# Second attention layer: relative rows and score pieces of at most 256 columns put between the transposes of the current tile

## The chip, the cores and the metric

The kernel runs on one core of one Trainium2 chip. The metric is the device time of one execution in microseconds (us). Times in the profile are microseconds from the start of the profiled execution, unless marked ns. Engines: PE is TensorE's matmul side, PEld its weight loads, DVE VectorE, ACT ScalarE, POOL GpSimd, SP SyncE, which issues the DMAs.

## The reference, cut to what matters

Four layers run one after the other on x of shape (2, 1024, 128), each with a layer norm before and after and a residual: attention with 16 heads and shared logits, a mixture of 8 experts, attention with relative positions, and a feed-forward of composed weights. The change is in the third, called the second attention layer here:

```
q = (x @ Wq.T) as (B, 16 heads, T, 8);  k, v with 4 groups, each repeated for 4 heads
scores = (q / sqrt(8)) @ k
dist = clip(pos_k - pos_q, -127, 127) + 127
bias[b,h,q,k] = (q / sqrt(8))[b,h,q] . E[dist[q,k]]
attn = softmax(scores + bias);  out = (attn @ v) @ Wo.T
```

T is 1024, so the bias depends on the position only in a band of 255 distances around the diagonal; outside of it, it is one of two constants per query.

## The kernel before, in words

Function `attend` computes one batch element of this layer, and is called twice. It goes over 16 heads, and in each over 8 tiles of 128 queries: 128 tiles a call, 256 in all. `u = 8h + qt` numbers them. What happens to a tile:

1. `scores` (L331): TensorE multiplies the tile's queries (each number split into three bf16 parts, so the contraction is 72 rows) with all 1024 keys into psS. psS is 128 x 1024 f32 and there is one copy. Three variants of the keys lie in KT: the plain ones for the band, and two with the far constants folded in, for the columns left and right of it. `segments(qt)` says which columns use which variant, cut at 512 as well: 3 or 4 matmuls a tile, 26 a head. Before the first it waits for `s_z >= u`, that is, for VectorE to have read the scores of the tile before. The last one raises `s_s`.
2. VectorE (L439) adds the bias A to psS, writes Z (two copies) and takes the row minimum m (queries are negated), and raises `s_z`.
3. GpSimd (L467, L468) computes m - Z in place, and raises `s_sub`.
4. TensorE (L385) transposes Z in eight blocks of 128 columns with the f32 identity, four into each half of psT. Each half waits for ScalarE to have read it for the tile before, and raises `s_t` when done.
5. ScalarE (L496) takes the exp of each half into Pt (two copies), and raises `s_exp`.
6. `values` (L360) multiplies with the values on TensorE, 32 columns of weights at a time, one tile later.
7. In tiles 3 and 7 of a head, `to_rows` (L371) also folds four tiles' outputs; this document calls them fold tiles.

The bias band is made one head ahead. `relative(h + 1, qt, u + 8)` (L346) multiplies the next head's queries with the 512 rows of the band into psE, one copy of 128 x 512 f32. It waits for `s_rows >= u + 8`: ScalarE must have copied the previous psE. ScalarE's `gather` (L488) copies psE to `rows`, after both exps of the tile, and raises `s_rows`; SyncE stores it to DRAM and fetches it skewed into A, for use one head later. The last head of a batch has no relative matmul.

Each engine goes through its own instructions in the order written. TensorE's order in the loop over tiles (`head`) is: wait for `s_sub`; transposes of half 0, then of half 1; `scores` of tile u + 2; `relative` of tile u + 8; `values` of tile u - 1; the fold where there is one. ScalarE's is: exp of half 0, exp of half 1, copy of psE.

Of the kernel before, what the change touches and what calls it, by code (L numbers as in the profile page):

```python
# [6 lines left out]
P = 128  # L7
# [3 lines left out]
QT_N = N // P  # L11
H, DH = 16, 8
SPLIT = 3
KR = SPLIT * SPLIT * DH
# [278 lines left out]
def attend(nc, tag, b, QT, KT, gkv, V, A, attn, con, segments, rel=None):  # L293
# [8 lines left out]
    RPT = H // gkv  # L302
    idf, fold = con["idf"], con["fold"]
    with phase(nc, tag) as ph:
# [8 lines left out]
        psS = ph.pb("psS", [P, N])  # L313
# [13 lines left out]
        with nc.Block() as block:  # L327

            @block.tensor
            def _(pe):  # L330
                def scores(h, qt, u):  # L331
                    if not (type(u) is int and u == 0):

                        pe.wait_ge(s_z, u)
                    for var, k0, k1 in segments(qt):
                        kh = h if gkv == H else var * gkv + h // RPT
                        last = nc.tensor.matmul(psS[:, k0:k1], QT[0:KR, h, qt * P:(qt + 1) * P], KT[0:KR, kh, k0:k1],  # L337
                                                start=True, stop=True)
                    last.then_inc(s_s, 1)

                def relative(h, qt, v):

                    if not (type(v) is int and v == 0):

                        pe.wait_ge(s_rows, v)
                    nc.tensor.matmul(psE[:], QT[0:KR, h, qt * P:(qt + 1) * P], EBT[0:KR, :], start=True, stop=True).then_inc(s_e, 1)  # L346

                def values(h, qt, u, first):
                    g, t = qt // GS, qt % GS
                    if qt == 0:  # L350

                        pe.wait_ge(s_vh, h + 1)
                    if t == 0 and not first:

                        pe.wait_ge(s_os, h * 2 + (g - 1))

                    pe.wait_ge(s_exp, u * 2 + 2)
                    for kt in range(QT_N):
                        j = kt % 4
                        last = nc.tensor.matmul(psO[32 * j:32 * j + 32, g, t * P:(t + 1) * P], Vh[:, kt, :],  # L360
                                                Pt[:, qt % 2, kt * P:(kt + 1) * P], start=kt < 4, stop=kt >= 4)
                    last.then_inc(s_pv, 1)

                def to_rows(h, g, first=False):


                    pe.wait_ge(s_os, h * 2 + (g + 1))
                    if not first:
                        pe.wait_ge(s_div, h * 2 + g)
                    for t in range(GS):  # L370
                        last = nc.tensor.matmul(psF[:, t, 0:DH + 1], Os[:, g, t * P:(t + 1) * P], fold[:], start=True, stop=True)  # L371
                    last.then_inc(s_f, 1)

                def head(h, first=False, final=False):
                    for qt in range(QT_N):
                        u = h * QT_N + qt

                        pe.wait_ge(s_sub, u + 1)
                        for half in range(2):
                            if not (first and qt == 0):  # L380

                                pe.wait_ge(s_exp, u * 2 + (half - 1))
                            for k in range(4):
                                kt = half * 4 + k
                                last = nc.tensor.transpose(psT[:, half, k * P:(k + 1) * P], Z[:, qt % 2, kt * P:(kt + 1) * P], idf[:])  # L385
                            last.then_inc(s_t, 1)
                        if qt + 2 < QT_N:
                            scores(h, qt + 2, u + 2)
                        elif not final:
                            scores(h + 1, qt + 2 - QT_N, u + 2)  # L390
                        if rel and not final:
                            relative(h + 1, qt, u + QT_N)
                        if qt:
                            values(h, qt - 1, u - 1, first)
                        elif not first:
                            values(h - 1, QT_N - 1, u - 1, first)
                        if qt == 3 and not first:
                            to_rows(h - 1, 1)
                        if qt == 7:
                            to_rows(h, 0, first)  # L400

                if rel:
                    for qt in range(QT_N):
                        relative(0, qt, qt)
                scores(0, 0, 0)
                scores(0, 1, 1)
                head(0, first=True)
                with pe.Fori(1, H - 1) as h:
                    head(h)
                head(H - 1, final=True)  # L410
                values(H - 1, QT_N - 1, H * QT_N - 1, False)
                to_rows(H - 1, 1)
# [1089 lines left out]
```

## Time and profile before

| | |
|---|---|
| median of three runs | 1898.95 us (1897.33 to 1901.57) |
| the profiled execution | 1901.43 us |
| its span, first to last instruction | 1899.7 us |
| mean granted TensorE clock | 0.907 of full |
| busy: PE, PEld | 1552.7 us (82%), 1119.6 us (59%) |
| busy: DVE, ACT, POOL | 1053.9 (55%), 892.1 (47%), 821.5 (43%) |
| relative matmuls, L346 | 256, 101.2 us |
| score matmuls, L337 | 832, 157.5 us |

The attention of the second layer runs from about 1092 to 1424 and from about 1478 to 1810. "Busy" of PE adds the time in which at least one matmul is recorded, from its start to its modelled end; since one starts while another ends, a PE that is always busy may still have gaps in its stream. The groups of the profile name what ended an engine's idle time; "issue" means nothing that the profile shows. A weight load is a row of its own (PEld), started ahead of its matmul where it can be.

### The profile page before, as it was taken

What the parts mean: (1) busy time and instruction counts of PE and PEld (TensorE: products, weight loads), DVE (VectorE), ACT (ScalarE), POOL (GpSimd) and SP (SyncE); (2) the same over time, 40 slices, a digit from 0 to 9 for tenths busy, and PEclk for the clock granted to TensorE, in tenths of its full rate; (3) what the DMA queues carried; (4) which work ended last, traced back from release to release, by engine and by line L of the source; (5) the groups of instructions that cost most, each with busy time, mean ns of one, the idle gap of its engine ahead of it and who ended that gap; (6) DMA issues with size and microseconds to landing.
All of it is one profiled execution on the core that took longest, in us unless ns stands there. A gap on an engine that the chain in (4) does not pass through costs nothing. (4 is left out here: it accounts for less than half of the span.)

```text
span 1899.7 us, 46841 instructions
## 1 busy us (share of the span) xinstructions
PE 1552.7 (82%) x16823; PEld 1119.6 (59%) x16823; DVE 1053.9 (55%) x3049; ACT 892.1 (47%) x1558; POOL 821.5 (43%) x1298
## 2 busy tenths in 40 slices
PE   3799999879999993267970589999995899999935
PEld 2476666646766763145650457777774577777734
DVE  5666556476655655732324845666558455566552
ACT  2355455445555551002220367777753566666612
POOL 2266566426665640062450245555541355555500
PEclk9899999999999995588995789999996799999968
DMA  4000000000000000712531056555530555555400
GB/s 120 1 1 2 2 2 2 2 1 1 2 2 2 2 2 5 251 40 54 104 60 32 1 179 185 178 178 178 175 121 1 161 177 179 182 180 177 138 1 22
DMA packets 102762, 147.48 MB, mean 78 GB/s; under 512 B 11632, under 2 KB 59120, under 8 KB 102640
## 3 DMA queue, kind: packets, MB, share of 16 engines
q1 hardware_dynamic: 95856, 140.87, 23.8%
q0 software_dynamic: 6784, 4.87, 1.9%
q8 instruction: 90, 1.47, 0.3%
q14 instruction: 32, 0.26, 0.0%
HBM read 68.49 MB, written 77.21 MB: 77 GB/s over the span
## 5 line engine op out<-in xcount | busy, mean ns | idle before, releaser
L439 DVE CUSTOM_DVE_ANT_0 t_Z<-t_psS,a1b_A 128x1024 f32<-128x1024 f32 x256 | 312.4, 1220 | 202.3 <-issue 202.3
L657 DVE CUSTOM_DVE_ANT_0 t_Z<-t_psS,a0b_L 128x1024 f32<-128x1024 f32 x256 | 311.1, 1220 | 186.3 <-issue 183.0
L715 ACT ACTIVATE t_Pt<-t_psT 128x512 f32<-128x512 f32 x512 | 278.7, 595 | 253.8 <-PE t_psT L613 253.6
L496 ACT ACTIVATE t_Pt<-t_psT 128x512 f32<-128x512 f32 x512 | 278.3, 595 | 191.9 <-PE t_psT L385 191.9
L613 PE MATMUL t_psT<-idf,t_Z 128*128 128x128 f32 x2048 | 285.8, 284 | 8.1 <-issue 6.6
L680 POOL TENSOR_SCALAR t_Z<-t_Z,t_m 128x1024 f32<-128x1024 f32 x256 | 287.3, 1122 | 0.0
L468 POOL TENSOR_SCALAR t_Z<-t_Z,t_m 128x1024 f32<-128x1024 f32 x256 | 286.8, 1120 | 0.0
L385 PE MATMUL t_psT<-idf,t_Z 128*128 128x128 f32 x2048 | 282.0, 281 | 2.0 <-POOL t_Z L468 1.6
L613 PEld LDWEIGHTS t_psT<-idf,t_Z 128*128 128x128 f32 x2048 | 226.6, 144 | 59.4 <-issue 32.1
L385 PEld LDWEIGHTS t_psT<-idf,t_Z 128*128 128x128 f32 x2048 | 227.7, 144 | 42.5 <-issue 37.4
L467 POOL TENSOR_TENSOR t_touch<-t_m 128x1 f32<-128x1 f32 x256 | 49.4, 193 | 270.1 <-DVE t_m L439 268.2
L360 PE MATMUL t_psO<-t_Pt,t_Vh 128*32 128x128 f32 x4096 | 164.9, 279 | 0.0
L587 PE MATMUL t_psO<-t_Pt,t_Vh 128*32 128x128 f32 x4096 | 164.5, 280 | 0.3 <-ACT t_Pt L715 0.3
L488 ACT ACTIVATE t_rows<-t_psE 128x512 f32<-128x512 f32 x256 | 152.9, 597 | 16.7 <-PE t_psE L346 15.7
L570 PE MATMUL t_psS<-a0b_KT,a0b_QT 72*128 72x512 bf16 (+1 forms) x512 | 155.9, 387 | 5.7 <-PEq L74 4.1
L337 PE MATMUL t_psS<-a1b_KT,a1b_QT 72*128 (+4 forms) x832 | 157.5, 303 | 2.7 <-DVE t_m L439 2.7
L587 PEld LDWEIGHTS t_psO<-t_Pt,t_Vh 128*32 128x32 f32 x4096 | 97.0, 109 | 105.8 <-issue 81.6
L360 PEld LDWEIGHTS t_psO<-t_Pt,t_Vh 128*32 128x32 f32 x4096 | 96.3, 109 | 84.7 <-ACT t_Pt L496 56.7
L679 POOL TENSOR_TENSOR t_touch<-t_m 128x1 f32<-128x1 f32 x256 | 49.4, 193 | 195.3 <-DVE t_m L657 195.0
L346 PE MATMUL t_psE<-a_EBT,a1b_QT 72*128 72x512 bf16 x256 | 101.2, 395 | 13.8 <-ACT t_rows L488 10.0
L256 POOL COPY p_Kx<-p_parts 128x384 bf16<-128x384 bf16 (+1 forms) x96 | 43.9, 493 | 130.8 <-DVEq L231 130.8
L1161 POOL DMA_INDIRECT token_sums<-x_oe,x_xe x40 | 62.3, 1559 | 79.9 <-DVE x_oe L1026 67.7
(252 smaller groups left out, 1766.9 us busy)
## 6 DMA issues: line engine op xcount, KB each, us to landing
relative_rows<-t_rows SPq DMA_DIRECT2D x256, 256.0 KB, 2.0
a1b_A<-relative_rows SPq DMA_DIRECT2D x192, 192.0 KB, 2.5
a1b_A<-relative_rows SPq DMA_DIRECT2D x64, 128.0 KB, 2.3
x_B<-in_b SPq DMA_DIRECT2D x1, 4096.0 KB, 19.3
x_A<-in_a SPq DMA_DIRECT2D x1, 4096.0 KB, 26.7
expert_rows<-zp SPq DMA_DIRECT2D x1, 2740.0 KB, 12.7
x_xe<-expert_rows SPq DMA_DIRECT2D x8, 342.5 KB, 2.9
x_WP<-in_moe_pre SPq DMA_DIRECT2D x8, 256.0 KB, 3.4
```

Of the source, the lines that this page charges most:

```text
L337: last = nc.tensor.matmul(psS[:, k0:k1], QT[0:KR, h, qt * P:(qt + 1) * P], KT[0:KR, kh, k0:k1], start=True, stop=True)
L360: last = nc.tensor.matmul(psO[32 * j:32 * j + 32, g, t * P:(t + 1) * P], Vh[:, kt, :], Pt[:, qt % 2, kt * P:(kt + 1) * P], start=kt < 4, s ...
L385: last = nc.tensor.transpose(psT[:, half, k * P:(k + 1) * P], Z[:, qt % 2, kt * P:(kt + 1) * P], idf[:])
L439: nc.vector.tensor_tensor_reduce(out=Z[:, qt % 2, :], in0=psS[:], in1=A[:, qt, :], scale=1.0, scalar=3e38, op0=ALU.add, op1=ALU.min, accum ...
L468: nc.gpsimd.tensor_scalar(Z[:, qt % 2, :], Z[:, qt % 2, :], -1.0, m[:, qt % 2:qt % 2 + 1], ALU.mult, ALU.add).then_inc(s_sub, 1)
L496: nc.scalar.activation(Pt[:, qt % 2, half * (N // 2):(half + 1) * (N // 2)], psT[:, half, :], ACT.Exp).then_inc(s_exp, 1)
L570: last = nc.tensor.matmul(psS[:, j % 2, k0:k0 + 512], QT[0:KR, hq * J + j, qt * P:(qt + 1) * P], KT[0:KR, hq * J + j, k0:k0 + 512], start= ...
L587: last = nc.tensor.matmul(psO[32 * j:32 * j + 32, (qt % GRP) * P:(qt % GRP + 1) * P], Vh[:, kt, j, :], Pt[:, qt % 2, j, kt * P:(kt + 1) * ...
L613: last = nc.tensor.transpose(psT[:, half, k * P:(k + 1) * P], Z[:, j, kt * P:(kt + 1) * P], idf[:])
L657: nc.vector.tensor_tensor_reduce(out=Z[:, j, :], in0=psS[:, j % 2, :], in1=L[:, qt, :], scale=1.0, scalar=3e38, op0=ALU.add, op1=ALU.min, ...
L680: nc.gpsimd.tensor_scalar(Z[:, j, :], Z[:, j, :], -1.0, m[:, j:j + 1], ALU.mult, ALU.add).then_inc(s_sub, 1)
L715: nc.scalar.activation(Pt[:, qt % 2, j, half * (N // 2):(half + 1) * (N // 2)], psT[:, half, :], ACT.Exp).then_inc(s_exp, 1)
```

## The change: what it does

In `head`, the score matmuls of tile u + 2 and the relative matmul of tile u + 8 are no longer behind the eight transposes of tile u but between them. The segments are cut into pieces of at most 256 columns: 4 pieces in tiles 0 and 7 of a head, 5 in the others, 38 a head. The relative matmul goes behind the first transpose. The pieces go behind the last four or five transposes, one behind each, the last piece behind the eighth. The wait for `s_z` is at the first piece, `s_s` is raised by the last, `s_t` still by the fourth transpose of each half. What is computed is the same.

```diff
+                def pieces(qt):
+                    return [(var, k, min(k + 256, k1)) for var, k0, k1 in segments(qt) for k in range(k0, k1, 256)]
+
+                def scores(h, qt, u, part):
+                    if part == 0 and not (type(u) is int and u == 0):
                         pe.wait_ge(s_z, u)
-                    for var, k0, k1 in segments(qt):
-                        kh = h if gkv == H else var * gkv + h // RPT
-                        last = nc.tensor.matmul(psS[:, k0:k1], QT[0:KR, h, qt * P:(qt + 1) * P], KT[0:KR, kh, k0:k1],
-                                                start=True, stop=True)
-                    last.then_inc(s_s, 1)
+                    var, k0, k1 = pieces(qt)[part]
+                    kh = h if gkv == H else var * gkv + h // RPT
+                    ins = nc.tensor.matmul(psS[:, k0:k1], QT[0:KR, h, qt * P:(qt + 1) * P], KT[0:KR, kh, k0:k1], start=True, stop=True)
+                    if part == len(pieces(qt)) - 1:
+                        ins.then_inc(s_s, 1)
...
                             for k in range(4):
                                 kt = half * 4 + k
                                 last = nc.tensor.transpose(psT[:, half, k * P:(k + 1) * P], Z[:, qt % 2, kt * P:(kt + 1) * P], idf[:])
-                            last.then_inc(s_t, 1)
-                        if qt + 2 < QT_N:
-                            scores(h, qt + 2, u + 2)
-                        elif not final:
-                            scores(h + 1, qt + 2 - QT_N, u + 2)
-                        if rel and not final:
-                            relative(h + 1, qt, u + QT_N)
+                                if k == 3:
+                                    last.then_inc(s_t, 1)
+                                if kt == 0 and rel and not final:
+                                    relative(h + 1, qt, u + QT_N)
+                                part = kt - QT_N + len(pieces((qt + 2) % QT_N))
+                                if part >= 0 and qt + 2 < QT_N:
+                                    scores(h, qt + 2, u + 2, part)
+                                elif part >= 0 and not final:
+                                    scores(h + 1, qt + 2 - QT_N, u + 2, part)
```

Before the first head, the scores of tiles 0 and 1 are now issued in pieces too.

## Rows read from the trace of the kernel before

**Rows 1.** Busy time by stage: span, PE, PEld, DVE, ACT, POOL, clock, DMA.
```profile
1200.00:1220.00 20.00, 20.00 (x254) 14.75 (x256) 12.09 (x39) 14.95 (x27) 10.89 (x19) 1.00 0.58 178
```

**Rows 2.** Order of time, one tile: start, us, engine, line, operation, xcount, idle before.
```profile
1210.42 1.09 PE L385 MATMUL t_psT<-idf,t_Z 128*128 128x128 f32 x8
...
1211.11 1.09 ACT L496 ACTIVATE t_Pt<-t_psT 128x512 f32<-128x512 f32 x2 [0.56 <-PE t_psT L385]
...
1211.35 0.60 PE L337 MATMUL t_psS<-a1b_KT,a1b_QT 72*128 x4
...
1211.79 0.38 PE L346 MATMUL t_psE<-a_EBT,a1b_QT 72*128 72x512 bf16 x1
1212.01 1.22 DVE L439 CUSTOM_DVE_ANT_0 t_Z<-t_psS,a1b_A 128x1024 f32<-128x1024 f32 x1 [1.02 <-issue]
...
1212.10 0.64 PE L360 MATMUL t_psO<-t_Pt,t_Vh 128*32 128x128 f32 x16
1212.20 0.60 ACT L488 ACTIVATE t_rows<-t_psE 128x512 f32<-128x512 f32 x1
...
1212.67 1.09 PE L385 MATMUL t_psT<-idf,t_Z 128*128 128x128 f32 x8
...
1213.49 1.12 POOL L468 TENSOR_SCALAR t_Z<-t_Z,t_m 128x1024 f32<-128x1024 f32 x1
```

**Rows 3.** The same view, one head's length, with a fold (L371).
```profile
1200.52 1.09 PE L385 MATMUL t_psT<-idf,t_Z 128*128 128x128 f32 x8
...
1214.92 1.06 PE L371 MATMUL t_psF<-cf,t_Os 128*128 128x9 f32 x8
...
1220.32 1.09 PE L385 MATMUL t_psT<-idf,t_Z 128*128 128x128 f32 x8
```

**Rows 4.** The same view in windows of 0.1 us, from transposes to scores.
```profile
1211.24 0.10 PEld L337 LDWEIGHTS t_psS<-a1b_KT,a1b_QT 72*128 x1
...
1211.24 0.27 PE L385 MATMUL t_psT<-idf,t_Z 128*128 128x128 f32 x1
...
1211.35 0.33 PE L337 MATMUL t_psS<-a1b_KT,a1b_QT 72*128 x1
...
1211.52 0.15 PEld L337 LDWEIGHTS t_psS<-a1b_KT,a1b_QT 72*128 x2
...
1211.57 0.38 PE L337 MATMUL t_psS<-a1b_KT,a1b_QT 72*128 x2
```

**Rows 5.** The same view at half clock, from relative matmul to transposes.
```profile
1108.29 0.63 PE L346 MATMUL t_psE<-a_EBT,a1b_QT 72*128 72x512 bf16 x1
1108.29 0.23 PEld L385 LDWEIGHTS t_psT<-idf,t_Z 128*128 128x128 f32 x1 [0.28 <-issue]
...
1108.71 0.42 PE L385 MATMUL t_psT<-idf,t_Z 128*128 128x128 f32 x1
```

**Rows 6.** Line L346, what ended its engine's idle time: us, times, whole execution.
```profile
  ACT t_rows L488: 26.7, 28
```

**Rows 7.** Order of time, start-up of a batch, relative matmul and copy.
```profile
1093.04 0.60 ACT L488 ACTIVATE t_rows<-t_psE 128x512 f32<-128x512 f32 x1 [1.22 <-PE t_psE L346]
...
1093.69 0.39 PE L346 MATMUL t_psE<-a_EBT,a1b_QT 72*128 72x512 bf16 x1 [0.69 <-ACT t_rows L488]
1094.12 0.60 ACT L488 ACTIVATE t_rows<-t_psE 128x512 f32<-128x512 f32 x1 [0.48 <-PE t_psE L346]
```

**Rows 8.** The same view, reduce and the scores that wait for it.
```profile
1102.95 1.22 DVE L439 CUSTOM_DVE_ANT_0 t_Z<-t_psS,a1b_A 128x1024 f32<-128x1024 f32 x1 [11.35 <-issue]
...
1104.23 0.13 PEld L337 LDWEIGHTS t_psS<-a1b_KT,a1b_QT 72*128 72x128 bf16 x2 [2.03 <-DVE t_m L439]
```

**Rows 9.** The same view, the last head of a batch.
```profile
1408.09 0.86 PEld L385 LDWEIGHTS t_psT<-idf,t_Z 128*128 128x128 f32 x8 [0.37 <-POOL t_Z L468]
...
1410.13 1.09 PE L385 MATMUL t_psT<-idf,t_Z 128*128 128x128 f32 x8
```

**Rows 10.** Busy time by stage, as in rows 1.
```profile
1400.00:1420.00 20.00, 19.42 (x255) 14.70 (x255) 11.88 (x38) 10.12 (x19) 11.10 (x19) 1.00 0.25 75
```

More of the change, by code:

```diff
@@ L330, in _ @@
             def _(pe):
-                def scores(h, qt, u):
-                    if not (type(u) is int and u == 0):
+                def pieces(qt):
+                    return [(var, k, min(k + 256, k1)) for var, k0, k1 in segments(qt) for k in range(k0, k1, 256)]
+                def scores(h, qt, u, part):
+                    if part == 0 and not (type(u) is int and u == 0):
                         pe.wait_ge(s_z, u)
-                    for var, k0, k1 in segments(qt):
-                        kh = h if gkv == H else var * gkv + h // RPT
-                        last = nc.tensor.matmul(psS[:, k0:k1], QT[0:KR, h, qt * P:(qt + 1) * P], KT[0:KR, kh, k0:k1],
-                                                start=True, stop=True)
-                    last.then_inc(s_s, 1)
+                    var, k0, k1 = pieces(qt)[part]
[3 more added lines that the diff above has]
+                        ins.then_inc(s_s, 1)
                 def relative(h, qt, v):
@@ L404, in _ @@
                         relative(0, qt, qt)
-                scores(0, 0, 0)
-                scores(0, 1, 1)
+                for qt in range(2):
+                    for part in range(len(pieces(qt))):
+                        scores(0, qt, qt, part)
                 head(0, first=True)
```

## The prediction

> **What bounds the kernel now.** I read the granted clock first, then the page, then the busy time by stage, then single tiles in order of time. The second layer's attention holds two stretches of some 320 us, 256 tiles in all. In its steady part TensorE is busy for the whole of every 20 us, at full clock, while the other engines stand at 54 to 75% [rows 1]. That is a hint only, because a matmul's recorded time overlaps its neighbour's. The order of time gives the proof [rows 2]: the transposes of one tile start at 1210.42 and those of the next at 1212.67, and in between every step starts where the stream before it lets it: eight transposes (0.93 to the first score matmul), 1024 score columns (0.44), the relative matmul (0.31 to the values), the values (0.57). The sum is 2.25 us, and nothing in it is a wait for an engine: VectorE's reduce ends at 1213.23, 0.3 before the next scores; GpSimd's subtraction ends at 1214.61, 0.3 before the transposes due at 1212.67 + 2.25. The tile is bound by TensorE's stream, and two buffers with a single copy lie just under it: psS (scores to reduce) and psE (relative matmul to ScalarE's copy). A whole head takes 1220.32 - 1200.52 = 19.80 us [rows 3]; six plain tiles take 13.50 of it, so the two tiles with an output fold take 3.15 each.
>
> **What the change costs on TensorE itself.** No column is added. 26 score matmuls per head become 38, 12 more, each with its weight load. Does the alternation save anything? Transposes follow each other at 0.109 us (0.87 for eight). The last one starts at 1211.24; the weights of the first score matmul start to load in the same instant, yet that matmul starts only at 1211.35 [rows 4]. A bf16 weight load needs no more than the 0.05 seen between the load at 1211.52 and the next matmul at 1211.57. So the 0.11 is the transpose's own occupancy, and putting a matmul behind it wins nothing. Does it lose? At half clock a f32 load starts at the relative matmul's own start, and the first transpose follows 0.42 later, the 512 columns' own time [rows 5]; from f32 to bf16 the row above shows the same. I take zero for each switch. The nearest row that speaks otherwise is the 0.10 between the relative matmul's columns and the 32-column values (1211.79 + 0.21 = 1212.00 to 1212.10, [rows 2]), another shape. Where a piece has only 128 columns (0.05) the f32 load behind it (at most 0.11) may stick out by 0 to 0.054; nine such pieces per head, so 0.06 a tile at most, and I take that.
>
> A page of the Trainium skill says otherwise: TensorE: Matmul & The Clock Gate, sections on LDWEIGHTS and on the back-to-back gap, has a weight load at columns divided by 1.2 GHz (107 ns for 128), a 128-column matmul at some 56 ns, and the next weights loading during the running matmul. By that a transpose is bound by its load, and a 256-column piece would hide half of it. The trace has the same 0.11 but puts it on the matmul; the rule's result is the first rival below.
>
> **What moves: the relative matmul.** It goes from behind the scores to behind the first transpose. It waits for ScalarE to have copied the previous psE. In the kernel before, that wait ends last only in the start-up of each batch, 14 starts counted on the load and 14 on the matmul [rows 6]; in steady state the copy (1212.20 to 1212.80) has until about 1214.0. ScalarE's order for a tile is exp of half 0, exp of half 1, copy, and it stays. The second exp waits for the eighth transpose, and now everything stands in front of that transpose: the relative matmul itself, six transposes, and all but one of the pieces. Behind the waiting relative matmul on TensorE stand all of them, and through them both exps: a ring.
> From the relative matmul's start R to the eighth transpose's start: 0.02 (a stalled start: a matmul of 0.39 against 0.38, [rows 2, 7]) + 0.213 for its 512 columns (half of the 0.42 at half clock, [rows 5]) + six transposes 0.654 + pieces before the last, 768 or 896 columns, mean 0.34 + 0.06 exposed loads = 1.29.
> From there: transpose to its end 0.27 [rows 4], to ScalarE 0.04 (1094.08 to 1094.12, [rows 7]), the exp 0.49 until the next activation can start (two take 1.08, one 0.60, [rows 2]), the copy 0.60, release 0.05 (1093.64 to 1093.69) = 1.45.
> Ring: **2.74 us against 2.25**. Unsure: whether the copy overlaps the exp as a second exp does; if not, 0.11 more.
> TensorE's own stream would be 2.25 + 0.06 = 2.31, so it idles 0.43 a tile. In the fold tiles the fold's 0.90 fills that: 3.15 + 0.06 = 3.21, the ring hidden. ScalarE's table load between heads of the first batch lands in such a tile.
>
> **psS, moved too.** The first piece takes the wait for the reduce, now with four transposes behind it. First piece to last piece: 0.33 columns + 0.44 transposes + 0.06, then 0.27 to its end, 0.06 to VectorE, 1.22 reduce, 0.06 release [rows 2, 8] = 2.44. That is over 2.25 as well, but under 2.74, so it is covered. It decides in the last head of each batch, which has no relative matmuls: before, tiles there come at some 2.05 (1408.09 to 1410.13, [rows 9]); 0.39 x 6 tiles x 2 = 4.7 us.
> GpSimd: reduce start to subtraction's end is 2.60 (1212.01 to 1214.61); over two tiles that needs less than 2.3 a tile, covered. The DMA requests come from copies that are later by the same amount; each tile's bias is needed most of a head later, covered. Pieces in the prologue (9 for 6): under a microsecond in all.
>
> **Sum.** Per head 6 x 2.74 + 2 x 3.21 = 22.86, less 19.80 = 3.06. 30 heads have relative matmuls: 91.8. Final heads 4.7. Together 96.5. The profiled execution took 1901.43 us (span 1899.7 and 1.7 around it), so it becomes 1997.9; it lies 2.5 over the median shown, so I say **1995 us**, 5% slower.
>
> **Rivals.**
> 1. *Alternation hides weight loads, but the ring holds.* If a transpose's 0.109 is its load and its matmul takes only 0.053 (the time of 128 columns at 1211.52, [rows 4]), a transpose plus a 256-column piece takes 0.16 for 0.216, and the load behind the relative matmul is hidden. R to the eighth transpose is 1.09, the ring 2.54, a fold tile 2.95, the head 21.14: +1.34 x 30 + 2 = +43, **1942 us**. For it: eight load starts at the same 0.109. Against it: 1211.24 to 1211.35. 8 in 100.
> 2. *Not slower.* The place is the same, the price per transpose t smaller still: a head is 17.20 + 52t (6 x 6 transposes in the ring, 2 x 8 in the fold tiles). It equals 19.80 at t = 0.050. Below that, with load and matmul both hidden behind pieces, the kernel gains: at 0.04, -0.52 x 30, **1883 us**. For it: 16 value matmuls of 128 columns do overlap in the array and take 0.57. Against: those use separate 32-column strips, the transposes all 128, and at 0.109 now they would have to lose more than half. 4 in 100.
> 3. *The clock falls.* TensorE now idles 0.43 in 2.74. At half clock the ring is 2.55 (the columns' times doubled) + 1.60 (a transpose 0.42, [rows 5]) = 4.15; a quarter of 240 tiles so: +85, **2080 us**. Against it: the last heads had idle time of 0.37 in a tile [rows 9], and in the 20 us from 1400 on, which hold that head, the granted clock was still full [rows 10]. 3 in 100.
> 4. *Each switch between f32 and bf16 costs.* 0.10 for each of four pieces would be +0.4 a tile, +72: **2067 us**. 3 in 100.
>
> **How the numbers follow.** The forecast gets 82 in 100, with its own range 1975 (no load exposed, copy started with more overlap) to 2020 (copy behind the exp: 0.11 x 180 = 20 us). To take in the first rival the range goes down to 1938, and up to 2030. A measurement of this kernel tells 0.2% (4 us) from nothing. Faster: 3 in 100, of rival 2; within 0.2%: 1; slower: 96, the rest.
>
> **What will show it.** The matmul of psE should stand behind the first transpose with a wait ended by ScalarE's copy in nearly every plain tile, some 180 or more, where it was none. Its start to the eighth transpose should be 1.3, that to the next relative matmul 1.45. Plain tiles should come every 2.74, fold tiles every 3.2, TensorE's granted clock full, VectorE's and GpSimd's idle time longer without being the cause. The transposes should still be 0.109 apart where nothing is between, and 0.21 to 0.22 with a 256-column piece; 0.16 is rival 1. If the last head's tiles come at 2.4 with the reduce as releaser, the psS part is right. The forecast is wrong if the relative matmul doesn't wait, or if the wait is there and the tile is still under 2.5.

## The result, and the profile after

| | before | after |
|---|---|---|
| median | 1899.66 us (4 runs) | 2003.7 us (4 runs, 2002.87 to 2005.19) |
| ratio to before | 1 | 1.0549 (95% interval 1.0533 to 1.0566) |
| span of the profiled execution | 1899.7 us | 2002.2 us |
| mean granted TensorE clock | 0.907 | 0.906 |

The change costs 5.5%, some 104 us; 1995 us had been forecast. In the tables below, "+us" is a ratio less one, times 1900, so that kernels measured beside different runs of the kernel before can be compared.

The page's first line gives instructions and busy time of each engine:

```profile
PE 1597.3 (80%) x17207; PEld 1161.3 (58%) x17207; DVE 1054.2 (53%) x3049; ACT 893.2 (45%) x1558; POOL 821.5 (41%) x1298
```

These are 384 matmuls more, and every other engine has as much to do as before. PE's busy time rises by 45 us, though no column is added. A matmul's recorded time of 0.27 lasts past the start of the next one, so each place where the stream stops leaves a tail of it that counts as busy. It is the stops and not the alternation: the last kernel below alternates and hardly waits, and has 1558.7 us; the one that only moves the relative matmul, and waits for it, has 1586.5. In a steady stretch (busy time by stage, columns as in [rows 1]) PE now has holes, and each other engine does less per microsecond:

```profile
1220.00:1240.00 20.00, 18.31 (x224) 13.78 (x223) 10.55 (x34) 12.77 (x23) 9.27 (x17) 1.00 0.47 148
```

Compared with [rows 1], all engines slow down together at full clock: that is a longer cycle, not a busier engine. The order of time shows it for a plain tile; these rows answer to [rows 2]:

```profile
1224.70 0.10 PEld L349 LDWEIGHTS t_psE<-a_EBT,a1b_QT 72*128 x1 [0.50 <-issue]
1224.70 0.39 PE L349 MATMUL t_psE<-a_EBT,a1b_QT 72*128 72x512 bf16 x1 [0.32 <-ACT t_rows L494]
...
1224.93 0.49 PE L388 MATMUL t_psT<-idf,t_Z 128*128 128x128 f32 x3
...
1225.26 0.27 PE L340 MATMUL t_psS<-a1b_KT,a1b_QT 72*128 x1
...
1225.37 0.27 PE L388 MATMUL t_psT<-idf,t_Z 128*128 128x128 f32 x1
...
1225.48 0.27 PE L340 MATMUL t_psS<-a1b_KT,a1b_QT 72*128 x1
...
1225.99 0.27 PE L388 MATMUL t_psT<-idf,t_Z 128*128 128x128 f32 x1
...
1226.25 0.64 PE L363 MATMUL t_psO<-t_Pt,t_Vh 128*32 128x128 f32 x16
1226.30 0.60 ACT L502 ACTIVATE t_Pt<-t_psT 128x512 f32<-128x512 f32 x1 [0.24 <-PE t_psT L388]
...
1226.79 0.59 ACT L494 ACTIVATE t_rows<-t_psE 128x512 f32<-128x512 f32 x1
1226.82 0.14 PEld L388 LDWEIGHTS t_psT<-idf,t_Z 128*128 128x128 f32 x1 [0.20 <-issue]
...
1227.52 0.10 PEld L349 LDWEIGHTS t_psE<-a_EBT,a1b_QT 72*128 x1 [0.56 <-issue]
...
1227.53 0.39 PE L349 MATMUL t_psE<-a_EBT,a1b_QT 72*128 72x512 bf16 x1 [0.37 <-ACT t_rows L494]
```

Read it as a ring. The relative matmul starts at 1224.70, the eighth transpose at 1225.99 (1.29 later), the second exp at 1226.30, the copy of psE at 1226.79; it ends at 1227.38, and the next relative matmul starts at 1227.52. The first transpose of the next tile was there at 1226.82; then TensorE stood still. The weight load's row says "issue" for the wait; only the matmul's row names ScalarE. The line's own view, which had 28 waits, all in the start-up [rows 6], now has:

```profile
  ACT t_rows L494: 94.1, 220
```

That is 192 more: 180 matmuls, six in each of 30 heads, and 12 loads, those of the first head of each batch, whose rows name ScalarE too. The rows above are of a ring of 2.82; the others are 2.76 to 2.83 from matmul to matmul, and with a fold in between 3.18. One head, from one relative matmul of tile 0 to the next, takes 23.05 us where [rows 3] had 19.80:

```profile
1221.80 0.13 PEld L349 LDWEIGHTS t_psE<-a_EBT,a1b_QT 72*128 x1
```
```profile
1244.85 0.13 PEld L349 LDWEIGHTS t_psE<-a_EBT,a1b_QT 72*128 x1
```

In the last head of a batch, without relative matmuls, the other ring shows; these rows answer to [rows 9]:

```profile
1457.62 0.10 PEld L340 LDWEIGHTS t_psS<-a1b_KT,a1b_QT 72*128 72x128 bf16 x1 [0.41 <-DVE t_m L445]
1460.03 0.10 PEld L340 LDWEIGHTS t_psS<-a1b_KT,a1b_QT 72*128 72x128 bf16 x1 [0.41 <-DVE t_m L445]
```

The weight load of the first score piece stands idle for 0.41 until VectorE's reduce is done, and tiles come 2.41 apart.

The 104 us add up from the trace: 28 heads at 3.26 more (91 us), the two last heads at 1.3 more (3 us), and the way from the first relative matmul of a batch to its first fold, 38.5 and 38.3 us where it was 33.2 and 33.7 (10 us). That first way lies in part at half the clock (granted 0.50) in both kernels.

### The profile page after: what moved, and what is told of

The parts are those of the page before. It is cut to its first block and busy times, and to the rows that moved or that the text cites. A ratio compares the mean times of both kernels' runs of the same rounds, so it can differ in the third digit from the quotient of the medians.

```text
span 2002.2 us, 47721 instructions
## 1 busy us (share of the span) xinstructions
PE 1597.3 (80%) x17207; PEld 1161.3 (58%) x17207; DVE 1054.2 (53%) x3049; ACT 893.2 (45%) x1558; POOL 821.5 (41%) x1298
## 5 line engine op out<-in xcount | busy, mean ns | idle before, releaser
L502 ACT ACTIVATE t_Pt<-t_psT 128x512 f32<-128x512 f32 x512 | 305.8, 598 | 297.9 <-PE t_psT L388 297.8
L388 PE MATMUL t_psT<-idf,t_Z 128*128 128x128 f32 x2048 | 418.5, 282 | 1.9 <-POOL t_Z L474 1.9
L721 ACT ACTIVATE t_Pt<-t_psT 128x512 f32<-128x512 f32 x512 | 278.6, 595 | 251.3 <-PE t_psT L619 251.1
L388 PEld LDWEIGHTS t_psT<-idf,t_Z 128*128 128x128 f32 x2048 | 285.1, 145 | 74.6 <-issue 38.1
L619 PE MATMUL t_psT<-idf,t_Z 128*128 128x128 f32 x2048 | 284.2, 283 | 7.5 <-issue 6.5
L340 PE MATMUL t_psS<-a1b_KT,a1b_QT 72*128 (+2 forms) x1216 | 269.4, 261 | 3.9 <-DVE t_m L445 3.7
L619 PEld LDWEIGHTS t_psT<-idf,t_Z 128*128 128x128 f32 x2048 | 225.2, 144 | 59.3 <-issue 31.8
L340 PEld LDWEIGHTS t_psS<-a1b_KT,a1b_QT 72*128 (+1 forms) x1216 | 121.5, 100 | 7.7 <-DVE t_m L445 6.7
```

The lines of the kernel that those rows point to most:

```text
L340: ins = nc.tensor.matmul(psS[:, k0:k1], QT[0:KR, h, qt * P:(qt + 1) * P], KT[0:KR, kh, k0:k1], start=True, stop=True)
L502: nc.scalar.activation(Pt[:, qt % 2, half * (N // 2):(half + 1) * (N // 2)], psT[:, half, :], ACT.Exp).then_inc(s_exp, 1)
L721: nc.scalar.activation(Pt[:, qt % 2, j, half * (N // 2):(half + 1) * (N // 2)], psT[:, half, :], ACT.Exp).then_inc(s_exp, 1)
```

## The experiments

The theory under test: two rings through buffers with one copy, psE's and psS's, and the longer one sets the tile. A ring here is the way from one use of a buffer, through everything that must happen before it is free, to the next use. The rivals: alternating transposes and score pieces costs TensorE time by itself; or the psE wait is the whole cause.

Each ratio is to runs of the kernel before that were taken beside it.

| kernel | ratio (95%) | +us |
|---|---|---|
| the change | 1.0549 (1.0533 to 1.0566) | 104 |
| pieces between, relative last | 1.0266 (1.0246 to 1.0287) | 51 |
| relative first, scores whole and behind | 1.0215 (1.0195 to 1.0234) | 41 |
| split only | 1.0036 (1.0021 to 1.0051) | 7 |
| the change, copy of psE before the exps | 1.0252 (1.0228 to 1.0276) | 48 |
| as above, two transposes inside the pieces | 1.0067 (1.0049 to 1.0085) | 13 |
| the change, TensorE's head loop written out | 1.0456 (1.0428 to 1.0485) | 87 |
| before, loop written out | 0.9999 (0.9988 to 1.0009) | 0 |
| split only, loop written out | 0.9985 (0.9975 to 0.9995) | -3 |
| short rings and loop written out | 1.0034 (1.0022 to 1.0046) | 6 |

### Pieces between the transposes, relative matmul last

Against the changed kernel:

```diff
                                 if k == 3:
                                     last.then_inc(s_t, 1)
-                                if kt == 0 and rel and not final:
-                                    relative(h + 1, qt, u + QT_N)
...
                                     scores(h + 1, qt + 2 - QT_N, u + 2, part)
+                        if rel and not final:
+                            relative(h + 1, qt, u + QT_N)
```

> The changed kernel, but with the relative matmul behind the last piece, where it stood before; the pieces stay between the transposes. Two-ring theory (psE ring 2.8 us a tile, psS ring some 2.5 under it): the psE wait is gone, the psS ring decides. First to last piece 0.33 + 0.44, then 0.27 + 0.06 + 1.22 + 0.06 to 0.14 release = 2.38 to 2.46 and up to 0.06 of exposed loads: plain tiles at 2.4 to 2.5, a head 6 x 2.47 + 2 x 3.17 = 21.2, 30 heads +41, last heads +4: 1945 us (1930 to 1958). Rival 'the alternation costs TensorE time by itself': stays near the changed kernel, 1990 or more. Rival 'only the psE wait counts': back to the kernel before, 1900.

1951.38 us, +51. The psE wait is back to its 28 times, and this ring decides (order of time; first piece, last piece, reduce, next first piece):

```profile
1222.30 0.10 PEld L340 LDWEIGHTS t_psS<-a1b_KT,a1b_QT 72*128 x1 [0.28 <-issue]
...
1223.11 0.27 PE L340 MATMUL t_psS<-a1b_KT,a1b_QT 72*128 x1
...
1223.44 1.22 DVE L445 CUSTOM_DVE_ANT_0 t_Z<-t_psS,a1b_A 128x1024 f32<-128x1024 f32 x1 [1.28 <-issue]
...
1224.80 0.10 PEld L340 LDWEIGHTS t_psS<-a1b_KT,a1b_QT 72*128 x1 [0.28 <-issue]
```

From the first piece it is 0.81 to the last piece, 0.33 to the reduce, 1.22 in it, and 0.14 from its end at 1224.66 to the next load: 2.50. The psS ring is real and is worth half of the loss alone. Both rivals fall: the alternation is all there and half of the loss is gone; the psE wait is gone and half of the loss is still there.

### Relative matmul first, scores whole

Against the kernel before:

```diff
                                 last = nc.tensor.transpose(psT[:, half, k * P:(k + 1) * P], Z[:, qt % 2, kt * P:(kt + 1) * P], idf[:])
+                                if kt == 0 and rel and not final:
+                                    relative(h + 1, qt, u + QT_N)
...
                             scores(h + 1, qt + 2 - QT_N, u + 2)
-                        if rel and not final:
-                            relative(h + 1, qt, u + QT_N)
```

> The kernel before with one edit: the relative matmul behind the first transpose. The scores are whole segments behind the eighth transpose. Two-ring theory: the psE ring is start of the relative matmul to eighth transpose 0.23 + 6 x 0.11 = 0.89, then 1.53 as seen after the change (transpose 0.27, 0.04, exp 0.49, copy 0.59, release 0.14) = 2.42 for 2.25: +0.17 x 6 x 30 = +31: 1930 us (1918 to 1942), with a wait for the copy in every plain tile. Rival 'the alternation costs': nothing alternates but one matmul, at most +0.1 a tile and no wait: 1900 to 1920.

1941.78 us, +41 where 31 were expected, and at the upper end of the range. Copy, relative matmul, transposes, exps, next copy:

```profile
1220.78 0.61 ACT L488 ACTIVATE t_rows<-t_psE 128x512 f32<-128x512 f32 x1
...
1221.52 0.10 PEld L346 LDWEIGHTS t_psE<-a_EBT,a1b_QT 72*128 x1 [0.23 <-issue]
...
1221.75 0.93 PE L385 MATMUL t_psT<-idf,t_Z 128*128 128x128 f32 x7
...
1222.28 1.08 ACT L496 ACTIVATE t_Pt<-t_psT 128x512 f32<-128x512 f32 x2 [0.89 <-PE t_psT L385]
...
1223.25 0.60 ACT L488 ACTIVATE t_rows<-t_psE 128x512 f32<-128x512 f32 x1
```

The load starts 0.13 behind the copy's end in the rows shown, so the wait is there, though its row says "issue". The cycle is 2.47, not 2.42. The eighth transpose starts at 1222.41, as computed, but the second exp starts at 1222.77, held up by the first exp and not by the transpose; the ring here goes through the fourth transpose and both exps. So one moved instruction, with no piece of the scores touched, costs 2%. Of the 10 us of miss, 0.05 x 6 x 30 = 9 are this exp.

### Split only

Against the changed kernel, so that the order is that of the kernel before:

```diff
-                                if kt == 0 and rel and not final:
-                                    relative(h + 1, qt, u + QT_N)
-                                part = kt - QT_N + len(pieces((qt + 2) % QT_N))
...
+                        for part in range(len(pieces((qt + 2) % QT_N))):
+                            if qt + 2 < QT_N:
+                                scores(h, qt + 2, u + 2, part)
+                            elif not final:
+                                scores(h + 1, qt + 2 - QT_N, u + 2, part)
+                        if rel and not final:
+                            relative(h + 1, qt, u + QT_N)
```

> Order of the kernel before, but the scores in pieces of at most 256 columns (38 matmuls a head for 26), all behind the eighth transpose, then the relative matmul. Two-ring theory: the 12 extra matmuls a head are only their fixed part, some 0.003 to 0.005 each: +1 to 2 us, 1901 (1897 to 1906). Rival 'splitting costs': 0.05 for each extra weight load would be +19, 1919.

1907.81 us, +7, between the theory's 1 to 2 (its range ended at 1906) and the rival's 19. In the trace a head takes 19.95 us where it was 19.79, so the steady heads account for some 4 of the 7. In some tiles the relative matmul's load comes only after the pieces are through, where it was 0.1 ahead before:

```profile
1223.28 0.60 PE L340 MATMUL t_psS<-a1b_KT,a1b_QT 72*128 x4
1223.76 0.10 PEld L349 LDWEIGHTS t_psE<-a_EBT,a1b_QT 72*128 x1
```

The four pieces' columns are over at 1223.28 + 0.43 = 1223.71. What delays the load is tried below.

### Copy of psE before the exps

Against the changed kernel:

```diff
                     for qt in range(QT_N):
                         u = h * QT_N + qt
+                        if rel and not final:
+                            gather(u + QT_N, qt % 4, h * 32 + (32 if qt < 4 else 48))
                         for half in range(2):
...
-                        if rel and not final:
-                            gather(u + QT_N, qt % 4, h * 32 + (32 if qt < 4 else 48))
```

> The changed kernel with TensorE's order untouched; only ScalarE copies psE before the two exps of a tile, not behind them. Two-ring theory: from the relative matmul's start 0.43 to the copy, 0.60, 0.14 = 1.2 us, so its wait is never last, and the psS ring is left: the same as pieces between with the relative matmul last, 1945 us (1930 to 1960). Rival 'TensorE's alternating stream is the cause': 2000, as ScalarE's order would not matter. Rival 'only psE counts': 1905.

1947.18 us, +48. Not one instruction of TensorE is different from the changed kernel, and 56 of 104 us are gone. The copy now starts 0.42 after the relative matmul, and the first piece waits for the reduce (ends 1224.58):

```profile
1223.36 1.22 DVE L445 CUSTOM_DVE_ANT_0 t_Z<-t_psS,a1b_A 128x1024 f32<-128x1024 f32 x1 [1.11 <-issue]
...
1223.97 0.38 PE L349 MATMUL t_psE<-a_EBT,a1b_QT 72*128 72x512 bf16 x1
...
1224.39 0.60 ACT L494 ACTIVATE t_rows<-t_psE 128x512 f32<-128x512 f32 x1 [0.51 <-PE t_psE L349]
...
1224.72 0.10 PEld L340 LDWEIGHTS t_psS<-a1b_KT,a1b_QT 72*128 x1 [0.17 <-issue]
```

This is the same level as with the relative matmul last, reached from the other side: under the psE ring lies the psS ring.

### The same, with two transposes inside the pieces

Against the changed kernel; the edit of ScalarE's order is the one just shown:

```diff
-                                part = kt - QT_N + len(pieces((qt + 2) % QT_N))
-                                if part >= 0 and qt + 2 < QT_N:
+                                np_ = len(pieces((qt + 2) % QT_N))
+                                parts = ([kt - (7 - 2)] if 7 - 2 <= kt < 7 else []) + (list(range(2, np_)) if kt == 7 else [])
+                                for part in parts:
...
```

> The changed kernel with both rings shortened: ScalarE copies psE before the exps, and only two transposes stand between the first and the last score piece (pieces behind the sixth, seventh, and all the rest behind the eighth). The relative matmul stays behind the first transpose. Two-ring theory: psE ring 1.2, psS ring 2.50 - 2 x 0.11 = 2.28, so TensorE's own stream of 2.25 to 2.3 decides again: the split kernel's level, 1907 us (1901 to 1916). If something else of the alternation costs (a third cause), it stays over 1920.

1916.75 us, +13, just above the range that was expected. It is 35 us less than with four transposes inside, so the ring's length counts about as computed (0.22 x 180 would be 40). It is 6 over the split kernel. One thing that is left in the trace: in two tiles of a head the relative matmul stands 0.2 behind the first transpose, here with its buffer free since 1224.74:

```profile
1225.84 0.33 PE L388 MATMUL t_psT<-idf,t_Z 128*128 128x128 f32 x1
1226.05 0.10 PEld L349 LDWEIGHTS t_psE<-a_EBT,a1b_QT 72*128 x1
```

### TensorE's loop over heads written out

```diff
-                with pe.Fori(1, H - 1) as h:
+                for h in range(1, H - 1):
                     head(h)
```

Three kernels have this edit: the change, the kernel before, and the split-only kernel.

> The changed kernel, with TensorE's loop over heads 1 to 14 written out, so that head numbers are constants and no register instruction stands between a wait and its weight load. Everything else as it was. Theory 'the release of 0.14 instead of the 0.05 of the start-up is register work after the wait': the psE ring falls by 0.09, 6 plain tiles x 28 heads: -15 us against the changed kernel, 1988 (1984 to 1993). Rival 'the 0.14 is the wait itself in a busy engine': no change, 2003 (2000 to 2006).

> The kernel before, with TensorE's loop over heads 1 to 14 written out in the same way. No wait ends last in its plain tiles, so the theory has no gain to give: 1900 us (1897 to 1903). If register work bounds TensorE's stream in some tiles, a little faster, down to 1890, and it would be the best kernel so far.

> The scores in pieces behind the eighth transpose, as in the split-only kernel (1907.8), with TensorE's loop over heads written out. Theory 'the 7.6 us of splitting are register instructions of the extra pieces (a relative matmul's load comes 0.05 late in tiles with them)': 1900 to 1902. Rival 'they are the extra matmuls' own fixed part': stays at 1906 to 1908.

1990.48, 1902.56 and 1900.0 us: by the ratios -17, 0 and -10 us against each one's looped form. By the traces a head goes from 23.05 to 22.56 us in the changed kernel, which is 14 us in 28 heads, stays at 19.79 in the kernel before, and goes from 19.95 to 19.81 in the split-only kernel, 4 us in 28 heads. The rest of the last one's 10 us was not located. In the changed kernel with its loop written out, copy and next relative matmul (the copy ends at 1225.01):

```profile
1224.42 0.59 ACT L494 ACTIVATE t_rows<-t_psE 128x512 f32<-128x512 f32 x1
...
1225.06 0.10 PEld L349 LDWEIGHTS t_psE<-a_EBT,a1b_QT 72*128 72x128 bf16 x1 [0.47 <-ACT t_rows L494]
```

The release takes 0.05 where it took 0.14. So the 0.09 is the loop's. With the head's number in a register, there are register instructions in TensorE's queue. In the looped form each relative matmul of heads 1 to 14 has one, of 46 ns:

```profile
L349 PEldq FUSED_REGOPS  x224: 46/46/70, 1129.2 to 1886.4; - x112
```

It is this instruction that holds the wait: for the relative matmul at 1227.52 it starts at 1227.42, 0.04 behind the end of the copy, lasts 0.05, and the weight load follows 0.05 behind its end. With the loop written out there is none, and the weight load holds the wait itself. The score line has 728 of them after the change and 616 before, fewer than its matmuls; the split-only kernel has 728 too. Where nothing waits, in the kernel before, they cost nothing. The split kernel's 0.9985 is the fastest seen, too close to 1 to be a gain worth having.

### Short rings and the loop written out

The edits of the last two sections together.

> All three causes taken away at once, with the relative matmul still behind the first transpose and pieces of at most 256 columns: ScalarE copies psE before the exps, two transposes inside the score pieces, TensorE's loop over heads written out. Theory (psE ring, psS ring, register work, nothing else): psS ring 2.28 - 0.09 = 2.19 and psE ring 1.1, both under TensorE's stream of 2.25 to 2.26 a tile: the level of the kernel before, 1900 us (1896 to 1905). If alternating two kinds of matmul costs something of its own, 1907 or more; if it saves TensorE time, under 1893.

1908.55 us, +6. That is over the theory's range and over the 1907 from which on the alternation was to have a cost of its own. The kernel to compare with is the split-only one with its loop written out, at ratio 0.9985: the difference is 9 us. The eight transposes, the relative matmul and the pieces of one plain tile (first transpose, values, next first transpose):

```profile
1218.37 0.33 PE L388 MATMUL t_psT<-idf,t_Z 128*128 128x128 f32 x1
...
1220.06 0.65 PE L363 MATMUL t_psO<-t_Pt,t_Vh 128*32 128x128 f32 x16
...
1220.63 0.33 PE L388 MATMUL t_psT<-idf,t_Z 128*128 128x128 f32 x1
```

These are 1.69 and 0.57, together 2.26 against 1.68 and 0.57 [rows 2]. From 1160 to 1400 the plain tiles take 2.264 on average, against 2.246 in the split-only kernel written out, and the fold tiles 3.23 against 3.17; the last heads take 0.4 more each. Part of that is still the psS ring. In one fold tile of each head the first piece waits for the reduce:

```profile
1222.62 1.23 DVE L447 CUSTOM_DVE_ANT_0 t_Z<-t_psS,a1b_A 128x1024 f32<-128x1024 f32 x1
...
1223.29 0.71 PE L388 MATMUL t_psT<-idf,t_Z 128*128 128x128 f32 x5
...
1223.91 0.10 PEld L340 LDWEIGHTS t_psS<-a1b_KT,a1b_QT 72*128 72x128 bf16 x1
```

The reduce ends at 1223.85; the last of the five transposes starts at 1223.72, so the piece was due at 1223.83 and comes 0.08 late. The same wait stands in four tiles of each last head. Without these, what the alternation costs TensorE itself is at most 0.02 a tile, some 4 or 5 us in all, and it saves nothing. GpSimd's subtraction, which now ends 0.12 before the transposes, is not in the way: the first transpose starts 0.20 behind the last value matmul in both kernels.

## Why the prediction was right, and where its sizes were off

- **The psE ring** was forecast at 2.74 and came at 2.76 to 2.83, 2.78 on average; a fold tile at 3.21 came at 3.18, a head at 22.86 at 23.05. It is shown by the wait, which stands in six tiles of each of the 30 heads, and by the copy moved ahead of the exps, which alone gives back 56 us.
- **Relative matmul to eighth transpose**, forecast at 1.29 as a mean, came at 1.22 to 1.29, 1.25 on average; the rows shown are of the longest. Of its terms, 0.06 for loads that stick out behind pieces of 128 columns was too much: the transpose behind such a piece starts 0.06 later and the next step 0.12 later, 0.01 lost. Against that, every step of the alternation is 0.111 to 0.113 instead of 0.107 to 0.109.
- **Eighth transpose to next relative matmul** was mis-sized: 1.45 forecast, 1.53 measured. The exp and the copy were right (0.49, 0.59), and that the copy overlaps the exp like a second exp is confirmed. The step that was off is the release, 0.05 taken from the start-up, where head numbers are constants; inside the loop it is 0.14. At 0.09 x 6 tiles x 28 heads = 15 us it is larger than the whole miss of 8.7. The stretch before it, 0.04 shorter than forecast, gave back 7 us, the fold tiles 2 and the last heads 2. That errors of both signs met is luck; the mechanism is not.
- **The start of a batch** was counted as a head like the others and costs 3 us more in all: 10 us for two first heads instead of 6.5. In its first tiles the granted clock is 0.50, and the psE ring takes 3.94 there (1103.91 to 1107.85).
- **The psS ring**, 2.44: 2.41 in the last heads, 2.50 inside the loop with the same 0.09. "Covered by the psE ring" was right, and it is why neither ring alone explains the time: alone they cost 41 and 51, together 104, since with both edits the pieces lie inside the psE ring too and lengthen it. The last heads cost 1.3 each (from the last fold before them to their end 20.42 and 21.70) and not 2.4: only four of their tiles have the wait, the others end on the fold or have no scores left to issue.
- **No saving from alternation**: right, and with it rivals 1 and 2 are out. A transpose and a 256-column piece take 0.22 (1225.26 to 1225.48), not 0.16. A transpose is not bound by its weight load: with a matmul of 0.107 between, the next transpose still holds the array for 0.11. The load alone takes far less here: behind a 128-column piece it is ready after 0.06.
- **Rival 3**, the clock: TensorE stood still for 0.4 us in each plain tile, and the granted clock stayed at 1.00 in the steady stretches (2.4 GHz). Only the stretches at half clock at the start of the two batches are longer, 27.3 us each where they were 17.1 and 23.9; whether the change does that was not tried.
- **Rival 4**, a price on each switch between f32 and bf16: at most 0.02 a tile. Out.
- **A slip in a reading**: VectorE's reduce ends 0.37 before the next scores in [rows 2], not 0.3. Nothing rests on it.

## What to carry to other kernels

Before an instruction is moved forward on an in-order engine, write down the ring that its buffer makes: the wait, everything that is now queued behind it until the consumer can start, the consumer's own queue, and the release. With one copy of the buffer that sum is the shortest possible iteration, whatever the engines' busy times say; here psE's had 1.2 us of slack where it stood, and it was moved forward by 1.2 us and put ahead of what frees it. Filling gaps between matmuls pays only if there are gaps: look at two neighbouring starts and at what the weight load between them really takes first.

## What the runs showed of the hardware that had not been expected

- A wait inside a loop is released later for a matmul that uses the loop's register: 0.14 us from the end of ScalarE's copy to the weight load, against 0.05 with a constant. The wait sits on a register instruction of 0.05 us ahead of the load. It costs nothing where the queue does not wait.
- A f32 weight load of 128 columns is recorded at 0.14 and spaced 0.11 in a row of transposes, yet behind a 128-column bf16 piece the transpose's matmul starts 0.06 after the load did. The spacing in the row is the matmul's.
- Two activations in a row overlap by 0.1 (starts 0.49 apart, 0.6 long), whether exp and exp or exp and copy; for exp and copy the prediction had left it open.
